# Attention and expert layer on one core: ScalarE instead of VectorE writes the high halves of the next batch's inputs

## The reference, cut to what matters

```python
# x, ctx: (8, 512, 512) f32; 16 heads of 32; 8 experts, top 2, capacity ceil(1.2 * 4096 / 8) = 615
Q = layernorm(x) @ Wq.T + bq;  K = ctx @ Wk.T + bk;  V = ctx @ Wv.T + bv   # per head
attn = softmax(Q @ K.T / sqrt(32));  x = x + tanh(g_xattn) * (attn @ V @ Wo.T + bo)
probs = softmax(layernorm(x) @ Wr + br);  gates, ids = top_k(probs, 2)     # routing with capacity
h = silu(xg @ W1 + b1);  y = (h @ W2 + b2) * gate                          # per expert
x = x + tanh(g_ffn) * scatter_add(y)
```

## Time and profile before

| | |
|---|---|
| median of 3 runs | 1959.96 us (1959.57 to 1960.15) |
| profiled execution | 1961.34 us, its span 1959.6 us |
| TensorE busy | 1788.7 us, 91% of the span |
| VectorE busy | 1167.3 us, 60% |
| ScalarE busy | 780.9 us, 40% |
| GpSimd busy | 484.3 us, 25% |
| mean granted TensorE clock | 0.964 of full speed |

### The profile page before, as it was taken

How to read it: one execution, slowest core, us unless ns; L and a number is a source line. 1 busy time by engine, 2 the same in 40 slices (tenths; PEclk the granted TensorE clock), 3 DMA queues, 4 the chain that set the end, 5 groups by cost and what they waited for, 6 DMA issues and landing times.

```text
span 1959.6 us, 30460 instructions
## 1 busy us (share of the span) xinstructions
PE 1788.7 (91%) x10822; PEld 919.9 (47%) x10822; DVE 1167.3 (60%) x2163; ACT 780.9 (40%) x1012; POOL 484.3 (25%) x451
## 2 busy tenths in 40 slices
PE   7999999999999999999811799999999999999996
PEld 4334242332424334242200566667676767666664
DVE  5777868777686777867587453635354443534330
ACT  5443634445354443634430342515161524334240
POOL 2313333232333313331141121221212211112101
PEclk9999999999999999999955899999999999999998
DMA  6214123150322414023130153433334342424311
GB/s 223 84 44 151 45 94 100 48 166 22 127 66 82 133 43 153 19 73 100 37 141 1 48 141 72 149 77 121 102 96 124 82 140 50 154 66 138 70 45 25
DMA packets 138205, 178.97 MB, mean 91 GB/s; under 512 B 45492, under 2 KB 86592, under 8 KB 134056
## 3 DMA queue, kind: packets, MB, share of 16 engines
q1 hardware_dynamic: 97192, 157.85, 24.7%
q0 software_dynamic: 40960, 20.41, 6.0%
HBM read 134.08 MB, written 43.63 MB: 91 GB/s over the span
## 4 chain that ended last, share of the span: by engine, by line
PE 83%; DVE 9%; ACT 3%; issue 2%; DMA 2%; SPq 1%; POOL 1%; DVEq 0%; ACTq 0%; POOLq 0%
PE psum L1445 21%; PE psum L1422 20%; PE psum L1158 7%; PE psum L1255 6%; PE psum L1262 6%; PE psum L1246 5%; PE psum L1236 5%; PE psum L1335 4%; PE psum L1273 4%; DVE mx L831 2%; PE psum L1163 2%; ACT osum L717 1%; DMA qk_rows<-qks 1%; PE psum L1398 1%; DVE cmp L980 1%
## 5 line engine op out<-in xcount | busy, mean ns | idle before, releaser
L1445 PE MATMUL psum<-w,hT 128*123 128x512 f16 x1920 | 420.3, 379 | 0.0
L831 DVE TENSOR_REDUCE mx<-psum 128x1 f32<-128x512 f32 x512 | 328.5, 684 | 153.4 <-PE psum L1236 152.6
L1422 PE MATMUL psum<-xgT,w 128*128 128x308 f16 (+1 forms) x3072 | 411.3, 294 | 0.6 <-DVE xgT L1089 0.6
L1422 PEld LDWEIGHTS psum<-xgT,w 128*128 128x128 f16 x3072 | 298.4, 97 | 109.7 <-DVE xgT L1089 0.8
L1445 PEld LDWEIGHTS psum<-w,hT 128*123 128x123 f16 x1920 | 257.9, 135 | 148.8
L709 ACT ACTIVATE pt<-psum 128x1024 f32<-128x1024 f32 x256 | 259.3, 1022 | 171.0 <-PE psum L1246 171.0
L759 ACT ACTIVATE h<-psum,b1c 128x308 f32<-128x308 f32 (+1 forms) x256 | 118.1, 512 | 379.4 <-PE psum L1422 379.0
L1107 DVE TENSOR_TENSOR hT<-h,hT 128x615 f16<-128x615 f32 x128 | 102.6, 801 | 212.2 <-ACT hT L762 212.1
L629 POOL DMA_INDIRECT out_dram<-y,idx_now x40 | 98.9, 2473 | 499.6 <-DVE y L1142 273.9
L1236 PE MATMUL psum<-stk 96*128 96x512 f16 x512 | 171.7, 384 | 20.0 <-DVE mx L831 18.9
L1158 PE MATMUL psum<-actT,wT 128*128 128x512 f16 x768 | 168.6, 381 | 2.0 <-DVE wT L818 2.0
(11 more groups left out here) (181 smaller groups left out, 1682.1 us busy)
## 6 DMA issues: line engine op xcount, KB each, us to landing
stage<-in_L_ffn_W_dram SPq DMA_DIRECT2D x64, 1024.0 KB, 5.0
stk<-qk_rows SPq DMA_DIRECT2D x192, 128.0 KB, 2.5
qk_rows<-qks SPq DMA_DIRECT2D x64, 256.0 KB, 2.6
xin<-in_x_dram SPq DMA_DIRECT2D x8, 1024.0 KB, 5.1
cin<-in_ctx_dram SPq DMA_DIRECT2D x8, 1024.0 KB, 5.1
xres<-in_x_dram SPq DMA_DIRECT2D x8, 1024.0 KB, 5.8
out_dram<-xres SPq DMA_DIRECT2D x32, 256.0 KB, 2.1
x_split<-x2hl SPq DMA_DIRECT2D x32, 256.0 KB, 2.3
```

Source lines behind the costliest of these rows:

```text
L831: v.reduce_max(mx[:, KT * t + qt:KT * t + qt + 1], ps, AX.X).then_inc(read, 1)
L1422: mm = t_.matmul(psum[:, (2 * m + ch) % 4, 0:c1 - c0], w1[:, wp, kt, m * P:(m + 1) * P], xgT[:, xp, kt, c0:c1], start=(kt == 0 and (wp, xp ...
L1445: mm = t_.matmul(psum[0:CP, Y_BANK[c], :], hT[:, hp, k, c * CP:(c + 1) * CP], w2[:, wp, k, :], start=(k == 0 and (hp, wp) == (0, 0)), stop ...
```

## The change

The high halves for batches 1 to 7 move from VectorE to ScalarE. VectorE's branch for them in `inputs_split` goes. `inputs_hi` takes the batch as an argument, and ScalarE calls it for the tiles of slot t in batches 0 to 6, behind the slot's exponentials and ahead of osum and aT. The low halves stay on VectorE, in their place.

```diff
-            def inputs_hi(n, kt):
+            def inputs_hi(b, n, kt):
 
-                ps, _ = filled(act, pre, ("actT", n, kt))
+                ps, _ = filled(act, act_use, ("actT", n, kt), b)
                 s.activation(actT[:, n, 0, kt, :], ps, ACT.Copy, scale=(1.0, SX)[n]).then_inc(act_hi, 1)
...
-                        inputs_hi(n, kt)
+                        inputs_hi(0, n, kt)
...
                             s.activation(pt[:, (2 * u + hf) % 4, :, :], psum[:, bank:bank + 2, :], ACT.Exp,
                                          scale=1.0 / (math.sqrt(HD) * SQ * SQ)).then_inc(read, 1)
+                    if not last:
+                        for i in act_tiles(t):
+                            inputs_hi(b + 1, i // KT, i % KT)
                     if t in GROUP_END[:-1]:
...
             def inputs_split(b, n, kt):
 
-                if not (isinstance(b, int) and b == 0):
-                    ps, _ = filled(dve, act_use, ("actT", n, kt), b)
-                    v.tensor_scalar(actT[:, n, 0, kt, :], ps, (1.0, SX)[n], None, ALU.mult).then_inc(act_hi, 1)
                 dve.wait_ge(act_hi, 2 * KT * b + (KT * n + kt + 1))
```

## The result

The changed kernel takes 2020.91 us (median of 6 runs, 2016.12 to 2022.84), the kernel before, run beside it, 1959.76 us (6 runs). The ratio is 1.031, 95% interval 1.0295 to 1.0322: 3.1% slower. The forecast was 2014 us.

A forecast was written before the change was run, and what follows sets the result against it. TensorE was taken to bound the kernel. Waits of 7 x 6.04 = 42.3 us plus clock falls of 11.8 us made 54.1, on 1961.34 giving 2015.4, less 1.4 for the median: 2014 us, range 1998 to 2028.

The forecast's parts named there:

- What bounds the kernel: TensorE holds 83% of the wait chain; relieving VectorE in the transposing stretch could give back at most 0.17 us a batch.
- The first loop: Slot 17: high part behind both exponentials delays low part, t, aT and osum; TensorE 2.35 us late per batch.
- The second loop: Slots 20 to 22: tile 7 waits on bank 0 for tile 5's low part; TensorE 6.04 us late, 2.35 included.
- The cover of the last aT: Output product's first three quarters hide the last aT and its low part; cover grows from 1.1 to 1.5 us.
- The clock: TensorE's clock falls after the slot 22 hole, costing 1.7 us a batch, 7 x 1.7 = 11.8 us.
- case (b): Rival: TensorE's clock falls after both loops, 2014 + 11.8 = 2026 us; chance 0.14.
- one fall a batch: Clock falls only behind slot 22's 3.6 us hole, longer than 2 us; bounds were 0 and 2 falls a batch.
- Rival (c): Only the first loop costs, tile 7's wait on bank 0 being shorter: 7 x 2.35 = 16.5, 1976 us; chance 0.07.
- Rival (d): ScalarE takes high parts ahead of its exponentials, t 1.4 us earlier in slot 17: 1959 to 1960 us; chance 0.07.
- The rule of the Trainium skill: VectorE up to about 3x faster per element: ScalarE high part up to 2.1 us, kernel near 2055 us; no chance.

The follow-up runs named there:

- e8: Changed kernel, high halves between the slot's two exponentials, tile 7 in bank 2, first two output tiles and first two Q/K projections swapped in banks 4 and 2: 1965.5 us.
- e1: Changed kernel, but ScalarE writes the high halves of tiles 1 and 2 only and VectorE keeps the other six (batches 1 to 7): 1976.61 us.
- e2: Changed kernel, but ScalarE writes the high halves of tiles 4 and 5 only and VectorE keeps the others (batches 1 to 7): 1997.19 us.
- e4: Changed kernel, with TensorE transposing tile 6 seven times more into the same bank in slot 22's hole (batches 1 to 7): 2003.03 us.
- e6: Changed kernel with tile 7 in bank 2 instead of bank 0 and the first two output tiles swapped in banks 4 and 2: 1998.18 us.
- e9: Changed kernel, with TensorE transposing tile 3 twice more into the same bank while it would wait for osum in slot 19 (batches 1 to 7): 2017.06 us.
- e5: Changed kernel with each high half on ScalarE placed between the slot's two exponentials instead of behind both: 1965.1 us.

## Why the prediction was right, and where it was off

- What bounds the kernel: right. VectorE's 37 us less of work bought nothing that any run shows; even e8, which has all of the relief and hardly any new wait, is slower than before.
- The first loop: worked out were aT at 357.08, osum at 360.04 and the values of unit 12 at 361.10; the changed kernel has, less 16.94, 357.06, 359.97 and 361.05. e1 alone gives 2.3 us a batch against 2.35.
- The second loop: aT 370.99 against 370.93, tile 7 374.85 against 374.74. e2 gives 3.7 us for it without a clock fall, and e4 6.0 for both. 7 x 6.04 = 42.3 was the sum; e4's seven batches lose 45.3, less 3.2 for its two clock falls, 42.1.
- The cover of the last aT held: the output product shows no wait, and the rest of the batch passed the lateness on whole.
- The clock: in the changed kernel it fell as forecast, once a batch and behind the second hole; the size of the term was off. The term was 1.7 us a batch, read from two falls in the trace of before; in the changed kernel it is 8.8 - 6.0 = 2.8 in most batches. The stretches at 0.83, 0.50 and 0.81 lack 3.4 us of full speed, twice what the falls of before lacked; about 0.5 of it lay in the hole, since by the 0.83 the clock fell some 1 us before the hole ended. Six batches with 1.1 each are the 6.6 us between 54.1 forecast and the 60.7 that the seven lost; batch 0 paid what the term said. My case (b), a second fall behind the first loop, would give nearly the same total and is not what happened: the stretches between the two holes show 1.00, in the other six batches too.
- The reason given for one fall a batch was weaker than its outcome. "The first is broken up by work" does not keep the clock up: in the four kernels with both of the first loop's waits in full (the changed one, e1, e4, e6) it fell behind that loop in 4 of 28 batches. And the 2 us wait that was taken as the measure had no fall behind it in e8 and e9. That every batch of the changed kernel fell behind its second hole and none behind its first is in part luck: the rows of before could not promise it.
- Rival (c) is out by e6 and the 3.49 us wait. Rival (d), the high part taken ahead of the exponentials, comes nearest to e5, which has it ahead of the second one: it avoids the loops, as said, but is not a gain. t is not 1.4 us earlier either. This is VectorE in e5, third batch, slot 17:

```profile
355.91 0.69 DVE L810 SCALAR_TENSOR_TENSOR actT<-psum,actT 128x512 f16<-128x512 f32 x1 [1.33 <-ACT actT L655]
357.49 0.69 DVE L874 TENSOR_TENSOR t<-osum 128x512 f32<-128x512 f32 x1
```

The batch starts 3.19 us later than before, so this t stands at 354.30, 0.38 us behind the old 353.92: what VectorE saves on the high part it waits for ScalarE's. The high part ahead of both exponentials was not built.
- The rule of the Trainium skill that the prediction weighed ("ScalarE: Activation LUTs", section "Rules for kernel authors", its ratio given for bf16) did not bear on this f32 copy: ScalarE took 596 ns over 64 copies, not 2.1 us.

## What to carry to other kernels

When a producer and its consumer sit on one engine and one of them is moved, draw the two queues with everything that stands between: here 0.6 us of moved work closed a loop (high part behind the exponentials, low part behind it, the product t behind that, the next exponentials behind aT) worth 6 us a batch, and moving it ahead by one exponential in the queue took all but 1 us of that away. Price a hole in TensorE with the clock behind it, and take the price as a span (0 to 2.8 us here), not as the one value that a trace happens to show. A change of bank order has two neighbours: who held the bank before, and who takes it next.

## What the runs showed of the hardware

Behind a hole of TensorE of 3.5 us, the same one each time, the fall of the granted clock cost 2.8 us in most batches of the changed kernel, 1.6 us in most batches of e2, and nothing in one batch of e2. e9 shows all three values in one execution. In the changed kernel's third batch the clock fell before the hole had ended, in e2's behind its end. Holes of 1.14 and 1.27 us close together cost a fall of 1.5 to 1.8 us in 4 of 28 batches and nothing in the others. Transposes of f32 tiles, which produce nothing new, kept the clock up in the hole of slot 22: with them (e4) the eight values products behind it took 1.06 us, without them 1.94.
